# Mamba scan: spreads padded to 128 rows, and half of the second spread issued once more ahead of it

## The reference

```python
def _mamba(x, W_in, conv_w, conv_b, W_xp, W_dt, dt_b, A_log, Dp, W_out):
    xp, z = jnp.split(x @ W_in.T, 2, axis=-1)
    xc = silu(causal_conv4(xp) + conv_b)
    dt_lo, Bm, Cm = split(xc @ W_xp.T)          # R=8, N=64, N=64
    dt = jax.nn.softplus(dt_lo @ W_dt.T + dt_b)
    A = -jnp.exp(A_log)
    def step(h, inp):                           # over the L=256 tokens
        xt, dtt, Bt, Ct = inp
        dA = jnp.exp(dtt[:, :, None] * A)
        h = dA * h + (dtt * xt)[:, :, None] * Bt[:, None, :]
        return h, jnp.einsum('ben,bn->be', h, Ct)
    ...
    return ((y + xc * Dp) * silu(z)) @ W_out.T
x1, x2 = _mamba(xn, ...m1), flip(_mamba(flip(xn), ...m2))
```

## Time and profile before

| | |
|---|---|
| Runs | 4419.17, 4422.01, 4432.62 us, median 4422.01 |
| Profiled execution | 4426.82 us, of which the span of instructions 4425.0 |
| TensorE busy, mean granted clock | 3580.8 us (81%), 0.808 |
| VectorE, ScalarE, GpSimd busy | 3278.4, 2367.4, 2500.9 us |
| Scan of pass 1, first product to last scan | 2994.0 to 3603.6 us |
| Scan of pass 2 | 3709.3 to 4316.2 us |

### The profile page before, as it was taken

How to read it: one execution, slowest core, us unless ns; L and a number is a source line. 1 busy time by engine, 2 the same in 40 slices (tenths; PEclk the granted TensorE clock), 3 DMA queues, 4 the chain that set the end, 5 groups by cost and what they waited for, 6 DMA issues and landing times. The chain is left out here.

```text
span 4425.0 us, 81252 instructions
## 1 busy us (share of the span) xinstructions
PE 3580.8 (81%) x26013; PEld 2271.0 (51%) x26013; DVE 3278.4 (74%) x5820; ACT 2367.4 (54%) x5461; POOL 2500.9 (57%) x2256
## 2 busy tenths in 40 slices
PE   5888888888866786875879799657988986988995
PEld 3666666666644654664754577422434442444443
DVE  4777777777746855765630788588999977999995
ACT  2555555555533533542332566466666756666761
POOL 2555555555544514424310333439999955999991
PEclk6999999999977987877989899875666676566666
DMA  1000000000000000000000000027777735777760
GB/s 55 9 9 9 9 9 9 9 9 9 9 19 0 0 6 15 0 7 5 0 27 0 20 1 1 15 96 237 233 226 222 230 120 183 234 232 226 227 216 27
DMA packets 196676, 328.22 MB, mean 74 GB/s; under 512 B 96048, under 2 KB 126016, under 8 KB 194368
## 3 DMA queue, kind: packets, MB, share of 16 engines
q1 hardware_dynamic: 196288, 323.29, 23.9%
HBM read 304.30 MB, written 18.87 MB: 73 GB/s over the span
## 5 line engine op out<-in xcount | busy, mean ns | idle before, releaser
L3555 ACT ACTIVATE banks<-banks,alog 128x255 f32<-128x255 f32 x2048 | 788.2, 448 | 364.5 <-PE banks L3469 223.7
L3469 PE MATMUL banks<-dt_rows,selectors 96*128 96x510 bf16 x1024 | 507.6, 552 | 170.3 <-ACT banks L3555 95.0
L3644 DVE TENSOR_TENSOR_SCAN h<-banks,dBx 128x1024 f32<-128x1024 f32 x256 | 579.3, 2279 | 50.5 <-ACT banks L3555 47.6
L3622 POOL TENSOR_TENSOR dBx<-residual,b_by_state 128x1024 f32<-128x1024 f32 x256 | 597.4, 2354 | 33.7 <-POOLq L3615 16.6
L3622 POOL TENSOR_TENSOR norm_featmajor<-norm,b_by_state 128x1024 f32<-128x1024 f32 x256 | 597.9, 2356 | 4.7 <-DVE h L3644 2.3
L3644 DVE TENSOR_TENSOR_SCAN h<-banks,norm_featmajor 128x1024 f32<-128x1024 f32 x256 | 580.0, 2278 | 13.1 <-ACT banks L3555 8.4
L3484 PE MATMUL banks<-h,c_spread 128*32 128x128 f32 x8192 | 486.3, 379 | 10.0 <-DVE h L3644 7.8
L3484 PEld LDWEIGHTS banks<-h,c_spread 128*32 128x32 f32 x8192 | 275.3, 145 | 306.1 <-issue 256.7
L3469 PEld LDWEIGHTS banks<-dt_rows,selectors 96*128 96x128 bf16 x1024 | 139.8, 152 | 363.8 <-ACT banks L3555 275.9
L973 POOL TENSOR_TENSOR weighted<-probs,f 128x1024 f32<-128x1024 f32 x64 | 120.8, 1903 | 215.4 <-DVE f L1024 214.2
L2611 POOL TENSOR_TENSOR out_factors<-out_norms,exponents 128x4 f32<-128x4 f32 x64 | 64.5, 1008 | 288.7 <-DVE out_norms L2776 288.7
(11 more groups left out here) (451 smaller groups left out, 8847.5 us busy)
## 6 DMA issues: line engine op xcount, KB each, us to landing
residual<-mamba_dtx_rows SPq DMA_DIRECT2D x512, 256.0 KB, 3.5
norm<-mamba_dtx_rows SPq DMA_DIRECT2D x512, 256.0 KB, 3.4
mamba_dt_rows<-dt_parts SPq DMA_DIRECT2D x8, 768.0 KB, 3.4
dt_rows<-mamba_dt_rows SPq DMA_DIRECT2D x32, 192.0 KB, 4.9
delta_blocks<-A_turned SPq DMA_DIRECT2D x256, 8.0 KB, 1.5
inv_turned<-delta_blocks SPq DMA_DIRECT2D x256, 8.0 KB, 1.8
mamba_dtx_rows<-dtx SPq DMA_DIRECT2D x16, 256.0 KB, 3.6
c_spread<-in_l3a_zero SPq DMA_DIRECT2D x2, 1160.0 KB, 6.8
```

Of the source, the lines that this page charges most:

```text
L3469: nc.tensor.matmul(out, mem["sel"][:, row].rearrange("r n g -> r (n g)"), rows[:, kh, 2 * x:2 * x + 2, 1:], start=True, stop=True).then_in ...
L3555: e = fn(per_step(decay[l % 2])[:, 2 * x + j, 1:], k.bank[x][:, j * T + 1:(j + 1) * T], ACT.Exp, scale=mem["A"][:, at:at + 1])
L3622: nc.gpsimd.tensor_tensor(per_step(dBx[l % 4]), per_step(kept[l % 4]), across(mem["B"][:, tokens(tb)], 4), ALU.mult).then_inc(q["dbx"], 1)
L3644: v.tensor_tensor_scan(flat(h[:, u % 2, 4 * i:4 * i + 4, :]), decay[l % 2], dBx[l % 4], 0.0, ALU.mult, ALU.add).then_inc(q["scanned"], 1)
```

## The change

`dt_rows` and `selectors` get 128 rows in place of 96. Rows 96 to 127 of both are set to zero once, by POOL at the start of pass 1, and hold nothing else; so a spread multiplies 128 rows and returns the same. Copies and loads still write 96 rows. And ahead of the second spread of each iteration TensorE runs its first 255 columns once more, with the same weights into the same place of the bank, where the full spread then writes over it.

```diff
-    m["rows"] = p.sb("dt_rows", [SROWS, 2, 4, T], BF16)
+    m["rows"] = p.sb("dt_rows", [P, 2, 4, T], BF16)
...
-    m["sel"] = p.sb("selectors", [SROWS, 16, 64, SE], BF16)
+    m["sel"] = p.sb("selectors", [P, 16, 64, SE], BF16)
...
-                    sp.dma_start(mem["rows"][:, 0], mem["dt_rows"][:, 0:4, 0:T]).then_inc(mem["rows_in"][0], 16)
+                    sp.dma_start(mem["rows"][0:SROWS, 0], mem["dt_rows"][:, 0:4, 0:T]).then_inc(mem["rows_in"][0], 16)
...
                 if m == 1:
+                    nc.gpsimd.memset(mem["sel"][SROWS:P], 0.0)
+                    pool.drain()
+                    nc.gpsimd.memset(mem["rows"][SROWS:P], 0.0)
+                    pool.drain()
                     nc.gpsimd.tensor_copy(rev[:], k.HT[:, :, PAD + T - 1:PAD - 1:-1]).then_inc(q["reversed"], 1)
...
-                    v.tensor_copy(mem["sel"][:], mem["self"][:].unsqueeze(2).to_broadcast([SROWS, 16, 64, SE]))
+                    v.tensor_copy(mem["sel"][0:SROWS], mem["self"][:].unsqueeze(2).to_broadcast([SROWS, 16, 64, SE]))
...
                     out = k.bank[x].rearrange("p (j t) -> p j t", t=T)[:, :, 1:]
+                    if x == 1:
+                        nc.tensor.matmul(out[:, 0:1, :], mem["sel"][:, row].rearrange("r n g -> r (n g)"),
+                                         rows[:, kh, 2 * x:2 * x + 1, 1:], start=True, stop=True)
                     nc.tensor.matmul(out, mem["sel"][:, row].rearrange("r n g -> r (n g)"),
                                      rows[:, kh, 2 * x:2 * x + 2, 1:], start=True, stop=True).then_inc(q["cast"], 1)
```

More of the change, by code:

```diff
@@ L3438, in load_rows @@
                     sp.wait_ge(q["cast"], 4 * NI * v)
-                    sp.dma_start(rows[:, kh], mem["dt_rows"][:, 4 * kh:4 * kh + 4, tb * T:(tb + 1) * T]).then_inc(rows_in[kh], 16)
+                    sp.dma_start(rows[0:SROWS, kh], mem["dt_rows"][:, 4 * kh:4 * kh + 4, tb * T:(tb + 1) * T]).then_inc(rows_in[kh], 16)
                 def next_dtx(n):
```

## The result

| | before | changed |
|---|---|---|
| Median of 11 runs each (us) | 4429.04 (4419.17 to 4441.98) | 4397.40 (4392.57 to 4416.80) |
| Profiled execution (us) | 4426.82 | 4408.55 |
| TensorE busy (us), mean clock | 3580.8, 0.808 | 3422.4, 0.897 |

The ratio, estimated from all these runs, is 0.9936, with a 95% interval of 0.9921 to 0.9952: 21 to 35 us less (the two medians alone give 0.9929). The forecast was 4400 us. The clock is the granted share of full speed: of the fifty windows of 2 us between 3250 and 3350 us in the trace of before, 46 show 0.50 or 1.00, and I read a number between the two as a mean over time.

What follows compares the result with a forecast made beforehand. GpSimd (POOL) was taken to bound the scan passes. 19.1 us won inside them plus 5.6 at the ends, less 2.5 for zeroing, gave 22.2 off the 4422.0 median: 4400 us, range 4388 to 4425.

Steps and rivals of the forecast that it cites:

- POOL's losses inside the passes: POOL's waits between products in both scan passes: 25.8 us lost, 6.7 expected to remain, so 19.1 won.
- the two ends behind the last product: VectorE's last scan ends 4.5 and 5.7 us behind POOL's last product; could be 2.3 each, 5.6 us won.
- the zeroing: Two POOL memsets at the start of pass 1 delay VectorE's scalings: 0 to 3.6 us, taken as 2.5.
- The bound: In the scan passes POOL bounds; TensorE costs only what makes POOL wait, at most 25.8 us inside the passes.
- The clock rises in the turns, and the rows count: In iterations turning a unit's result, 2.5 spreads per 2.68 us, times 128/96 for rows, make 1.24, raising TensorE's clock.
- Rival 1: Clock stays down in iterations turning a unit's result, which take 2.68 us: 4472 us; chance 0.10.
- Rival 2: Clock rises in only part of the iterations turning a unit's result, mean 2.49 us: 4424 us; chance 0.11.
- The padding's price: In TensorE's spreads, 128 rows instead of 96 cost 0 for 1024 spreads, since time goes by columns.
- The half spread's price: One extra 255-column matmul per scan iteration: 0.21 us at slow clock, 0.11 at full, then covered by VectorE's 2.18.
- The jumps: Loop jumps, twice a pass, make VectorE 5.6 us late; slack absorbs 4.6, POOL loses 1.0 each, 4.0 in all.
- rival 3: Clock rises, but the longer loop body costs 2 us more per jump, all falling on POOL: 4409 us; chance 0.12.
- The late DMAs: In the scan passes POOL itself waits for a few late DMAs, 1.4 + 1.3 us; 2.7 us stay lost.

Runs made afterwards that it cites:

- e8: The padding without the half spread, zeroing behind POOL's long work, no SP wait for weights, TensorE's and ScalarE's loops written out: median 4396.81 us, 0.9909 of the kernel before.
- e5: The changed kernel with late zeroing and the whole second spread (510 columns) issued twice instead of its first half: 0.9935 of the kernel before.
- e1: The changed kernel without the half spread, so the padding alone: 0.9959 of the kernel before.
- e2: The kernel before plus the half spread alone, 96 rows, no padding or zeroing: 1.0046 of the kernel before.
- the repeats: The changed kernel profiled twice more, unchanged: profiled executions 4408.44 and 4411.47 us.
- e4: The changed kernel with late zeroing and the half spread only in the 16 iterations of a batch that hold a turn: 0.9933 of the kernel before.
- e6: The changed kernel with late zeroing and TensorE's batches 1 to 6 written out instead of looped: 0.9949 of the kernel before.
- e7: The changed kernel with late zeroing and without SP's wait for the second pass's weights in pass 1: 0.9933 of the kernel before.
- e3: The changed kernel with the two memsets moved behind POOL's three long operations, a drain ahead: 0.9947 of the kernel before.

## Why the prediction was right, step by step

| term | forecast (us) | measured, first profiles | measured, mean of three |
|---|---|---|---|
| POOL's losses inside the passes | -19.1 (25.8 to 6.7) | -14.9 (25.8 to 10.9) | -10.8 (20.5 to 9.7) |
| the two ends behind the last product | -5.6 | -5.4 | -6.2 |
| the zeroing | +2.5 | +3.5 | +3.6 |
| all else of the stage | 0 | -0.8 | +0.3 |
| the stage | -22.2 | -17.6 | -13.1 |

What POOL still lost in the changed kernel was forecast at 6.7 us and came out at 10.9. Late loads are 3.7 of it (2.7 forecast) and the jumps 3.7 (4.0 forecast). The other 3.4 us had no term in the prediction. They are spread thinly over the products: the 2.306 us of the first batch are not kept. In e8, without a jump, each batch behind the first is still 0.1 to 0.2 us longer, late load aside, 1.0 us a pass.

- **The bound.** Right. With the clock up, VectorE and POOL are busy for 36.00 of 36.00 us of the turns, and POOL's products pace the passes. Nothing could be won beyond 25.8 + 5.6 by the clock, and e5 shows that more of it wins nothing.
- **The clock rises in the turns, and the rows count.** Right, and shown by e1 and e2 in two ways: rows without the half spread raise it, the half spread without rows leaves it down in most turns. Counting spreads by number alone does not order the kernels: e1 has the number of before, 0.81 per us in the turns, and its clock rose, while e2 has 0.93 and stayed down in four of five turn iterations. Rival 1 had its place, its trigger and its cadence right; they come true when the padding is left out. Its price of 48 us was too high: e2's stage was 1546.20 us, 30.0 over the first profile of before, and this was the slowest of its executions; its timed runs are 10 to 31 us over before. The clock still rose in a fifth of the turn iterations (0.69 and 0.67 in the mean), and TensorE's stops at the jumps of pass 1 were 3.5 and 3.2 us, not 5. Rival 2 is not seen: in the turns' stretch the clock is 1.00, and in both passes the scans of the turns are 2.31 us apart in the median.
- **The size of the clock.** Forecast 0.9 for the passes, an estimate with no sum behind it; measured 0.94.
- **The padding's price.** Taken as 0, right: the spread takes 389 ns in the median and 376 at the least, as the fastest one did before.
- **The half spread's price.** 0.12 us measured for 0.11, covered as said. But it brings nothing either: e1 has no longer passes without it. The prediction took both parts as needed and could not tell them apart; that it had no number for the padding by itself is its weakest step.
- **The jumps.** The step "POOL loses of each jump 5.6 - 4.6 = 1.0 us" failed in size both ways. At those of pass 1 POOL had no wait, those of pass 2 cost it 2.06 + 1.66. That the sum, 3.7, is near the forecast 4.0 is luck. The slack of 4.6 us itself holds: 6.37 us late at VectorE gave 2.03 at POOL, 4.3 absorbed. What was off was the lateness. It is rival 3's mechanism in one pass of two. From scan to scan, pass 1 had 6.5 and 5.5 us at its jumps, pass 2 8.7 and 8.2; the repeats had 5.4, 5.6 and 8.9, 8.2, and 6.1, 5.9 and 7.4, 8.5. So the longer stops belong to the second pass's code and not to chance. e4, with shorter code, moved them to pass 1 (7.6 and 8.1, against 5.6 and 3.9), and the kernel before and e1 have second stops in pass 1 only, of 1.4 to 2.5 us. That they stem from the jump is shown by e6 and e8, where they go with the loop. That the engine waits there for code was not measured; it is my reading of the instruction packets, which lie there in all twelve profiles of kernels with the loop: one of 16384 bytes starts inside every first stop, and one within 1.2 us of the start of every second one. Why a body stops once or twice, by its length or by where it begins, stays open.
- **The late DMAs.** Forecast 2.7 us kept and measured 3.7, 2.5 and 3.4 in the three of the changed kernel, all at the start of batch 1 (in the second of the three the profile puts it down to the scan, not to the load). The cause is SP's wait for weights, shown by e7 (0.6 left); the prediction had left it unnamed.
- **The zeroing.** 3.5 us, the upper end of 0 to 3.6, where 2.5 was taken. The step that failed: the scalings did get their turn (1.97 us), as the lower end had it, but the engine's next work was then hit by the same POOL operations, shifted. The delay was passed on.

**What stays open.** By the traces the stage is 13.1 us shorter in the mean (10.7 to 17.8 by pair), and the blocks ahead of it are the same code. The timed runs say 21 to 35 us. The three profiled executions of the changed kernel (4408 to 4411) lie above its median of 4397.40, and those of before (4414 to 4427) below its 4429.04. So by the means of three, 8 us or more of the measured gain are in no trace here. They may lie ahead of the stage: the timed runs of the changed kernel spread over 24 us, while its stage keeps to 0.3. No run shows it.

**What was luck.** The forecast of 22 us less agrees with the runs, but in part because its base was the costliest of three profiles: with the mean of the three (20.5 lost inside the passes, 11.1 at the ends) the same working gives (20.5 - 6.7) + (11.1 - 4.6) - 2.5 = 17.8. And 4400 lies so close to 4397.40 because it was taken off 4422.0, the median of three runs of before; taken off that of eleven, 4429.0, the same 22.2 us give 4407.

## What to carry to other kernels

When TensorE is without idle time and its granted clock is still 0.50 (here 36.00 us busy of 36.00), look at how many rows its matmuls feed: here padding 96 rows with zeros to 128 raised it from 0.65 and 0.61 to 0.85 and 0.83 over the passes (e1), and cost nothing once the zeroing stood where POOL waits anyway (e3). Half a matmul more with 96 rows cost 0.5% of the time. Raise the clock only up to the point where the next engine bounds (here passes at 0.96, e5, were no shorter than those at 0.84, e1); then ask what that engine still loses, which here were loop jumps and one wait on the DMA queue. And profile the kernel before twice: the stage of this one, which went in and out of the full clock, varied by 6.9 us in three executions, and that of the changed kernel by 0.3.

## What the runs showed of the hardware

- Rows of zeros raised the clock: 96 rows to 128, with the two memsets and nothing else, raised the mean of a pass from between 0.61 and 0.66 (six passes of the kernel before) to between 0.83 and 0.85 (e1). Busy time does not order the two kernels: before, TensorE was busy 36.00 of 36.00 us of the turns at 0.50, and after 30.23 of 36.00 at 1.00. No run separates the rows of the weights (`selectors`) from those of the data (`dt_rows`), which were padded together.
- A POOL memset of 32 x 2048 bf16 takes 1.80 us (the first of the two 2.33), and one of 128 x 2048 f32 1.805 us: between these two, neither rows nor the width of an element changed it. VectorE's two tensor_scalar took 1.97 us beside the memsets and 0.5 without POOL, but 6.39 and 6.41 beside POOL's scaling of the input.
- A loop's jump stops TensorE for 3.2 to 5.5 us (48 jumps in twelve profiles), and in some bodies a second time, for 1.4 to 3.5 us, in the first iteration or just behind it. ScalarE has a stop of its own of 2.0 to 2.6 us (e6), seen once TensorE's was gone; at the first jump of the changed kernel it waits 5.06 us for TensorE instead. An instruction packet starts inside each of the 48 first stops and in ScalarE's four.
